# Attention scores in quarters of the array, plain products following their neighbours' tiling, and normalisations moved from GpSimd to ScalarE

## What is computed

```
# block 1, per sequence (H=16 heads of 8, R=8 values per head)
xn = LN(x); q, k, v, qv = four linear maps of xn
score = softmax(q k^T)                       # 16 heads, 512 x 512
out = score v ; comp = softmax over R of ([qv, out] Ws^T) ; out = sum(comp * out)
y = x + Wf out ; y = y + Wr2 relu(Wr1 LN(y)) ; x = LN(x + y)
# block 2, two layers (8 heads of 64, window 64 and the one before)
q, k = l2norm and rotary of h wqkv ; o = local softmax(8 q k^T + mask) v
x = x + wo o ; h = LN(shift(x)) ; x = x + w2 (a * gelu(g)), a, g = w1 h
# at the end x = LN(x_in + x)
```

## Time and profile before

| | |
|---|---|
| median of 3 runs | 1379.37 us (1377.97 to 1383.18) |
| profiled execution | 1383.29 us, its span 1381.5 us |
| TensorE busy | 1247.4 us (90%) |
| VectorE, GpSimd, ScalarE busy | 971.1, 901.7, 803.1 us |
| mean granted TensorE clock | 0.978 |

### The profile page before, as it was taken

One profiled execution on the slowest core, in us unless ns is written; L12 is line 12 of the kernel. 1 busy time (PEld: TensorE's weight loads), 2 busy tenths in 40 slices (PEclk: granted clock), 3 DMA queues, 4 the chain that ended last, 5 costly groups with the idle time before them and its releaser, 6 DMA issues.

```text
span 1381.5 us, 42047 instructions
## 1 busy us (share of the span) xinstructions
PE 1247.4 (90%) x17410; PEld 886.4 (64%) x17410; DVE 971.1 (70%) x1524; ACT 803.1 (58%) x1087; POOL 901.7 (65%) x886
## 2 busy tenths in 40 slices
PE   1689998999999999999999999999999999887885
PEld 1256765666867577666867577675767667565664
DVE  4777489788588876887678776877668673746452
ACT  1256765676656666666656666666656665544442
POOL 4003685778558783878657794778748693979373
PEclk9999999999999999999999999999999999998997
DMA  3410031112101121012111121012201001010100
GB/s 133 157 48 27 11 108 21 25 20 84 41 23 28 47 67 35 19 27 82 43 23 25 42 70 39 18 29 72 52 23 25 10 19 24 17 20 20 32 20 16
DMA packets 112972, 56.70 MB, mean 41 GB/s; under 512 B 82534, under 2 KB 105360, under 8 KB 112784
## 3 DMA queue, kind: packets, MB, share of 16 engines
q1 hardware_dynamic: 108288, 48.52, 13.5%
q10 hardware_dynamic: 4500, 5.51, 1.2%
HBM read 20.18 MB, written 14.68 MB: 25 GB/s over the span
## 4 chain that ended last, share of the span: by engine, by line
PE 77%; POOL 7%; DVE 6%; ACT 5%; issue 3%; DMA 1%; ACTq 1%; SPq 0%; POOLq 0%; DVEq 0%
PE pair L577 66%; PE pair L580 11%; POOL work L1130 3%; DVE gm L1013 2%; POOL rn L1130 2%; ACT probs L775 2%; ACTq L807 1%; ACT L775 1%; DVE o_tok L894 1%; ACT p_t L775 1%; DMA h<-yb 0%; DVE wm L1076 0%; DMA parts_scratch<-shared 0%; ACT work L775 0%; DVE wexp L894 0%
## 5 line engine op out<-in xcount | busy, mean ns | idle before, releaser
L1013 DVE TENSOR_REDUCE gm<-pair 128x2 f32<-128x1024 f32 x256 | 304.2, 1217 | 77.0 <-PE pair L577 74.6
L775 ACT ACTIVATE probs<-pair 128x1024 f32<-128x1024 f32 x256 | 253.8, 1024 | 40.9 <-PE pair L577 28.3
L577 PEld LDWEIGHTS pair<-vt,probs 128*64 128x64 f32 x8192 | 251.0, 138 | 34.5 <-issue 27.5
L577 PE MATMUL pair<-vt,probs 128*64 128x65 f32 x8192 | 268.0, 224 | 0.7 <-ACT gt L775 0.7
L577 PE MATMUL pair<-wqkv,h_t 128*128 128x512 f32 x384 | 188.5, 615 | 3.0 <-ACT h_t L775 1.4
L1130 POOL TENSOR_TENSOR rn<-rn,neg_half 128x16 f32<-128x16 f32 x64 | 187.6, 2932 | 5.3
L1130 POOL TENSOR_TENSOR work<-work 128x1024 f32<-128x1024 f32 (+1 forms) x65 | 151.3, 2328 | 1.0 <-DVE work L894 0.9
L894 DVE TENSOR_TENSOR work<-pair,rot 128x1024 f32<-128x1024 f32 x128 | 150.1, 1214 | 0.0
L775 ACT ACTIVATE raw<-pair 128x260 f32<-128x260 f32 x128 | 49.6, 388 | 142.0 <-PE pair L577 141.9
L1130 POOL TENSOR_TENSOR work<-work,rn 128x1024 f32<-128x1024 f32 x64 | 121.8, 1904 | 4.8
L577 PE MATMUL pair<-h_t,w 128*114 128x256 f32 (+1 forms) x384 | 110.2, 411 | 5.4 <-ACT probs L775 2.0
(11 more groups left out here) (146 smaller groups left out, 2367.4 us busy)
## 6 DMA issues: line engine op xcount, KB each, us to landing
v_mix<-v_nat SPq DMA_DIRECT2D x112, 128.0 KB, 2.8
parts_scratch<-shared SPq DMA_DIRECT2D x16, 384.0 KB, 2.6
k_stack<-parts_scratch SPq DMA_DIRECT2D x64, 96.0 KB, 2.2
q_stack<-parts_scratch SPq DMA_DIRECT2D x64, 96.0 KB, 2.3
parts_scratch<-shared SPq DMA_DIRECT2D x16, 256.0 KB, 2.7
x_in<-in_x SPq DMA_DIRECT2D x8, 256.0 KB, 2.7
parts_scratch<-shared SPq DMA_DIRECT2D x16, 128.0 KB, 2.5
h<-yb SPq DMA_DIRECT2D x64, 32.0 KB
```

The source lines that it names most:

```text
L577: return pe.matmul(b_out, lhsT, rhs, start=start, stop=stop, skip_group_check=True)
L775: return act.activation(dst, src, fn, **kw)
L1013: m = dve.tensor_reduce(gm[:, g % 2, j, :, s % 2], bank("max", b, s, j), AX, ALU.max, negate=True)
```

## The change

1. **Quarters.** `max`, `st` now issue each product as two column halves (`halves`), so that a task is four matmuls on 64 x 64 quarters, the form that `s` has already.
2. **Halves by neighbourhood.** A plain product is issued whole, or as two column halves (128 x 64) if the fixed-form task before it on TensorE is of the 128 x 64 kind (or, after a quarter task, the one that follows is). `gturn` reads 40 columns instead of 8, so that it has the 128 x 64 form too.
3. **The planner** knows three tilings (`TILING`), adds 93 ns to a start where the tiling changes (`RETILE`), shifts the rank of a task that would change it by -0.82 (`STAY`), lets ScalarE and VectorE be free 115 and 90 ns before their result is there, and has new offsets in `TAKEN` and new durations. So every engine's order is new.
4. **Normalisations.** `ln*_norm` goes to ScalarE as `Identity(scale * x + bias)`. GpSimd's `ln*_rstd` makes the bias too (minus mean times inverse root): four instructions instead of two.
5. **Loads.** The loads for block 1 go from ScalarE's queue to SyncE's (`load_search`); rotary tables and scales move to the 15 `layer_loads`, issued by SyncE in five groups after the last `stack` of sequence 0. A `warm` activation loads ScalarE's exponential table at the start.

```diff
+TILING = {"pv": "columns", "o": "columns", "h_turn": "columns", "gturn": "columns", "max": "both", "st": "both", "s": "both",
+          "x_turn": "whole", "att_turn": "whole", "n2_turn": "whole", "qkT": "whole", "pT": "whole", "oT": "whole",
+          "n_turn": "whole", "out_turn": "whole", "out_back": "whole"}
+RETILE = 93
+STAY = -0.82
+def retiles(tiling, wanted):
+    return tiling == "both" if wanted is None else tiling is not None and tiling != wanted
 TAKEN = {
-    "rem": -9.0, "ma": -8.98, "qk_feat": -8.56, "cos": -8.5, "weight": -8.19, "lsub": -7.11, "qk": -6.98,
...
+    "ln2_norm": -9.0, "rowmax": -8.88, "n_turn": -8.62, "lnl_rstd": -7.97, "wsub": -5.25, "mg": -0.09, "pT": 0.1,
...
+        lag = {"ACT": 115, "DVE": 90}.get(engine, 0)
+        self.info[name] = (engine, ns - lag, [a for a in after if a], take, frees, land + lag, table)
...
-                key = (max(start, now[engine]), rank[name])
+                other = engine == "PE" and retiles(tiling, TILING.get(name[0]))
+                key = (max(start, now[engine]), rank[name] + STAY * other)
...
+                if retiles(tiling, wanted):
+                    start += RETILE
+                    tiling = None
+                tiling = wanted or tiling
...
+        for k in (1, -1):
+            tiling = None
+            for name in self.orders["PE"][::k]:
+                tiling = TILING.get(name[0]) or (tiling if tiling != "both" else None)
+                self.halved.setdefault(name, tiling and tiling == "columns")
+                if self.halved[name] is None:
+                    del self.halved[name]
...
-            add(("max", b, s, j), "PE", 250, [("stack", b, 0, g), ("stack", b, 1, g), quad_before("gsplit", g, 2),
+            add(("max", b, s, j), "PE", 220, [("stack", b, 0, g), ("stack", b, 1, g), quad_before("gsplit", g, 2),
...
-    add(("ln3_rstd", b), "POOL", 1360, [("ln3_stats", b)])
-    add(("ln3_norm", b), "POOL", 3130, [("ln3_rstd", b)] + [n("ysum", b - 2, LAYERS - 1, hf) for hf in range(2)])
+    add(("ln3_rstd", b), "POOL", 1950, [("ln3_stats", b)])
+    add(("ln3_norm", b), "ACT", 1500, [("ln3_rstd", b)] + [n("ysum", b - 2, LAYERS - 1, hf) for hf in range(2)])
...
-        gb = sb("gb", [P, 2, T, 2, 2, 2], BF16)
+        gb = sb("gb", [P, 2, 8 * T + 32], BF16)
...
+                def halves(dst, lhsT, rhs, start=True, stop=True):
+                    for c0 in range(0, lhsT.shape[-1], 64):
+                        c1 = min(c0 + 64, lhsT.shape[-1])
+                        m = mm(dst[c0:c1], lhsT[:, c0:c1], rhs, start, stop)
+                    return m
...
+                    product = halves if p.halved.get(name) else mm
...
-                        m = mm(z, wqk[a], xf[:, :])
+                        m = product(z, wqk[a], xf[:, :])
...
-                            m = mm(z[:, r, :], qs[rr, s, j * P:(j + 1) * P], ks[rr, s, :])
+                            m = halves(z[:, r, :], qs[rr, s, j * P:(j + 1) * P], ks[rr, s, :])
...
-                            m = mm(z[:, r, :], ks[rr, s, j * P:(j + 1) * P], qs[rr, s, :])
+                            m = halves(z[:, r, :], ks[rr, s, j * P:(j + 1) * P], qs[rr, s, :])
...
+                def normal(dst, src, tiles, rstd):
+                    for j in tiles:
+                        m = A(dst[:, j, :], src[:, j, :], ACT.Identity, scale=rstd[:, 0, j:j + 1], bias=rstd[:, 1, j:j + 1])
+                    return m
...
+                    if kind == "warm":
+                        act.wait_ge(s_fills, 1)
+                        m = A(warmed[:, :], neg_half[:, 0:1], ACT.Exp)
...
-                        if name == ("gcopy", 0, 0):
-                            for dst, src in layer_loads:
-                                act.dma_start(dst, src).then_inc(s_layers, 16)
...
+                def scales(dst, mom, name):
+                    n, (r, nb) = dst.shape[2], (dst[:, 0, :], dst[:, 1, :])
+                    pool.tensor_scalar(r, mom[:, :, 1], EPS, None, ALU.add).then_inc(sem(name), 1)
+                    pool.tensor_scalar(nb, mom[:, :, 0], -1.0, None, ALU.mult).then_inc(sem(name), 1)
+                    pool.wait_ge(*upto(*name, short=2))
+                    TT(r, r, neg_half[:, 0:n], ALU.pow).then_inc(sem(name), 1)
+                    pool.wait_ge(*upto(*name, short=1))
+                    return TT(nb, nb, r, ALU.mult)
...
+                    elif kind == "load_layers":
+                        k, = ix
+                        for a in range(2):
+                            sp.wait_ge(*upto("stack", 0, a, QUADS - 1))
+                        for dst, src in layer_loads[3 * k:3 * k + 3]:
+                            sp.dma_start(dst, src).then_inc(s, 16)
```

More of the change, by code:

```diff
@@ L94, in order @@
         self.orders = {e: [] for e in engines}
-        self.bank_of, self.before, self.starts = {}, {}, {}
+        self.bank_of, self.before, self.starts, self.halved = {}, {}, {}, {}
         free, freed_by = [0.0] * 8, [None] * 8
@@ L110, in room @@
             return best and (best[0][0], best[1])
-        ends, gives, table = {}, {}, None
+        ends, gives, table, tiling = {}, {}, None, None
         waiting = {}
@@ L170, in order @@
         assert all(not n for n in waiting.values()), [k for k, n in waiting.items() if n][:9]
+        for k in (1, -1):
[5 more added lines that the diff above has]
+                    del self.halved[name]
         return now
 def plan_setup(p):
+    p.rank = -5.0
+    p.add(("load_first", 0), "ACT", 4000, land=2400)
+    p.rank = -4.8
+    p.add(("warm", 0), "ACT", 250, table="exp")
+    p.rank = -0.5
+    p.add(("load_search", 0), "SP", 4400, land=3400)
+    p.rank = 0.1
+    for k in range(5):
+        p.add(("load_layers", 0, k), "SP", 1400, [("stack", 0, a, QUADS - 1) for a in range(2)], land=6000)
     p.rank = -2.0
-    p.add(("weigh", 0), "DVE", 800)
+    p.add(("weigh", 0), "DVE", 700, [("load_first", 0)])
     p.rank = -1.9
@@ L248, in plan_search @@
         add(("gsplit", b, g), "POOL", 500, [("rowmax", b, *sj) for sj in here] + [quad_before("gturn", g, 2)])
-        add(("gturn", b, g), "PE", 230, [("gsplit", b, g), quad_before("gstack", g, 1)], "one", ("gcopy", b, g))
+        add(("gturn", b, g), "PE", 224, [("gsplit", b, g), quad_before("gstack", g, 1)], "one", ("gcopy", b, g))
         add(("gcopy", b, g), "ACT", 570, [("gturn", b, g)])
@@ L275, in plan_search @@
     step(1.02)
[L276 removed]
+    add(("att_turn", b), "PE", 440, [("attsum", b, hf, j) for hf in range(2) for j in range(T)] + [n("m1", b - 1, 1)],
         "one", ("att_feat", b))
@@ L319, in plan_local @@
             first = ("x_next", b, l - 1, hf) if l else ("ln3_norm", b)
-            add(("h_turn", b, l, hf), "PE", 500, [first, ("tables", 0), half_before("ma", l, hf, 2, 2)], "one", ("h_feat", b, l, hf))
+            add(("h_turn", b, l, hf), "PE", 494, [first, ("tables", 0), *[("load_layers", 0, k) for k in range(5)], half_before("ma", l, hf, 2, 2)], "one", ("h_feat", b, l, hf))
             add(("h_feat", b, l, hf), "ACT", 381, [("h_turn", b, l, hf)])
@@ L403, in transfers @@
         return (2 if kind == "v_mix" else 3) - (not more)
-    return {"spill": 3, "stack": 2, "gstack": 2}.get(kind, 1)
+    return {"spill": 3, "stack": 2, "gstack": 2, "load_layers": 3, "load_search": 9}.get(kind, 1)
 RAWC = RV + 1
@@ L559, in build @@
             (w_all[:, 2 * D:], t["w_all"][:, 2 * D:7 * D]),
-            (tab, t["tables"]), (flat[:, 1536:2048], t["scales"].partition_broadcast(P)),
         ]
-        layer_loads = [(mask[:, :, :], t["mask"])]
+        layer_loads = [(tab, t["tables"]), (flat[:, 1536:2048], t["scales"].partition_broadcast(P)), (mask[:, :, :], t["mask"])]
         for l in range(LAYERS):
@@ L1220, in _ @@
                         pool.wait_ge(*upto("ln3_stats", b))
-                        m = inverse_root(rstd2[:, :], moments2, name)
-                    elif kind == "ln3_norm":
-                        pool.wait_ge(*upto("ln3_rstd", b))
-                        if b > 1:
-                            for hf in range(2):
-                                pool.wait_ge(*upto("ysum", b - 2, LAYERS - 1, hf))
-                        m = normal(x_b[b % 2], s1, range(T), moments2, rstd2)
+                        m = scales(rstd2[:, :, :], moments2, name)
                     elif kind == "rnorm":
```

221 lines of the change are left out of this document (111 added, 110 removed).

## The result

The changed kernel takes 1418.84 us (median of 4 runs, 1416.09 to 1425.41) against 1381.11 for the kernel before on the same chip (4 runs): a ratio of 1.0273 [1.0245, 1.0302]. The forecast was 1344 us with a range from 1306 to 1374; the change has the wrong sign, and the time lies far outside the range. The profiled execution took 1425.4 us, its span is 1423.6.

The account below looks back on a forecast made before the run. TensorE's work was taken to bound the middle, latencies of chains the start and end. Terms -20 - 8 - 6 - 1 = -35 us took the profiled 1383.3 to 1348, or 1344 us against the 1379.4 median; range 1306 to 1374.

Parts of the forecast that it names:

- The new order: TensorE's list: the new planner would leave 60 fewer changes of tiling, -8 us, bounds +23 to -35.
- The prediction's own sign of being wrong: Profile after: the period stays above 155 us, or the first dense stretch starts over 5 us later than before.
- Quarters and halves: TensorE, old order: new forms cut changes of tiling from 875 to 709, saving leaving and entering costs, -20 us.
- Rival C: TensorE's score tasks: each shows one 104 ns load, 53 us over 512 tasks, time 1397 us; chance 0.06.
- Rival A: TensorE's list: the order does not keep tiling changes away; 1362 to 1386 us, say 1371; chance 0.21.
- Normalisations: Moved from GpSimd to ScalarE: hidden by TensorE's work in the middle, gaining at the end of the program, -6 us.
- rival D: ScalarE: waiting normalisations hold PSUM evictions that TensorE needs, +36 us, 1380, no change; chance 0.05.
- Loads: Program start: table load leaves the path, -2.5 us, against later gstack loads on SyncE's queue, +1.5; together -1 us.

Follow-up runs that it names:

- Experiment 5: The kernel before's planner with the new forms, only st planned at 218 ns instead of 250, orders made anew; 1482.53 us, ratio 1.0741 to the kernel before.
- experiment 1: The kernel before with its five orders unchanged and only the new forms (quarters, halves, gturn on 40 columns); 1356.01 us, ratio 0.9802.
- 12: New forms, block 1 loads on SyncE's queue, warm, and other TAKEN offsets whose plan still repeats, against the kernel before; 1359.19 us, ratio 0.9819.
- number 3: The changed kernel with its new orders, normalisations and loads, but the old forms: products whole, scores as 128 columns, gturn on 8; 1425.74 us, ratio 1.0302.
- 8: The changed kernel with STAY at nothing and the old TAKEN offsets, planned anew; 1430.27 us, ratio 1.0357 to the kernel before.
- 7: The kernel before with new forms and normalisations on ScalarE, planned there by the old planner with old offsets; 1446.29 us, ratio 1.0479.
- 6: The changed kernel with normalisations planned and run on GpSimd, every order made anew; 1436.27 us, ratio 1.0394 to the kernel before.
- experiment 2: The kernel before with new forms and normalisations moved to ScalarE's list at their planned starts, other orders kept; 1398.2 us, ratio 1.0108.
- Experiment 11: The kernel before's order with new forms, block 1 loads on SyncE's queue and warm; 1361.36 us, ratio 0.9836 to the kernel before.

## Why the prediction was wrong

**The step that failed is "The new order", -8 us with bounds of +23 and -35.** It priced an order by one property, its number of changes of form, because that was what the planner's edit spoke of. The number came out between its bounds (779, where it took 709 - 60), and by its own price of 0.14 us the miss is 130 x 0.14 = 18 us, of which 10 lie above the 709 of the old order. The rest of the cost is waits. The sum had order, normalisations and loads at -8 - 6 - 1 = -15 us together; measured, they cost 1418.84 - 1356.01 = 63. The old plan has settled into a cycle of one sequence in which TensorE was busy 152 of 157 us, and no rule of the planner asks for that. Whether the offsets in `TAKEN` were chosen with it is not on record; with `TAKEN` empty the same planner plans an end at 1460 us instead of 1292. Experiment 5 shows that the cycle is lost with one number, and 126 us with it, while the work stays the same. A new order had to be costed as a new draw, with a bound on the slow side from the row that was at hand: TensorE's 90%, kept by that one order. The prediction's own sign of being wrong, a period above 155 us, is what the steps of 158 to 181 us show.

**The plan told it.** The kernel computes its plan before it runs, so the planned starts of any version can be had without a run. The planned ends of block 2 are 149 us apart each time before, and 154, 164, 161, 171 after. The planned end of the whole program tells as much: 1292 us before and 1355 after, although most of TensorE's tasks are planned shorter. The table has it beside what was measured in the profiled executions. Tasks is the sum over TensorE's list of the distance from a task's start to the next one's, taken at the tenth percentile of all tasks of the same kind, form, and form before and behind; rest is the span less that sum, so waits and slow stretches.

| kernel | planned end | span | tasks | rest |
|---|---|---|---|---|
| before | 1292 | 1381.5 | 1201 | 181 |
| 1, new forms, old order | 1292 | 1356.3 | 1170 | 187 |
| 12, other offsets, repeats | 1290 | 1356.4 | 1170 | 186 |
| after | 1355 | 1423.6 | 1177 | 247 |
| 3, after with old forms | 1355 | 1426.2 | 1205 | 221 |
| 8 | 1369 | 1432.5 | 1158 | 274 |
| 7 | 1370 | 1444.6 | 1159 | 286 |
| 6 | 1372 | 1435.3 | 1178 | 258 |
| 5 | 1388 | 1478.4 | 1158 | 320 |

Computed in the same way, without a run, the old plan keeps its cycle with `st` at 248 to 251 ns and has lost it at 245 and 252. The plans that repeat end at 1290 to 1292, the others at 1355 to 1388, and the measured spans follow in nearly the same order. Number 5 has the least work on TensorE and the longest rest. From number 3 to the changed kernel the tasks lose 28 us and the rest gains 26. The split depends somewhat on how finely tasks are grouped: for the change as a whole it is -24 in the tasks and +66 in the rest here, and other groupings put the rest's growth between +43 and +72.

Part of the rest is the clock. Two successive short stretches in the middle of the changed kernel, the first with gaps in TensorE's work:

```profile
853.00:861.20 8.20, 6.07 (x108) 3.26 (x104) 8.16 (x12) 4.63 (x7) 7.87 (x8) 1.00 0.18 36
861.20:868.00 6.80, 6.10 (x24) 3.85 (x22) 4.96 (x6) 5.61 (x8) 6.63 (x4) 0.50 0.01 2
```

The granted clock goes to 0.50, the 1.2 GHz level, at 861.2 us, after 8.2 us in which TensorE was busy 6.07. The mean clock gives the size: 1423.6 x (1 - 0.946) = 77 us less 65 x 0.33 = 21 of the start, so 55 us of full-speed time lost, against 1381.5 x (1 - 0.978) = 30 before. That is up to 25 of the 66. The first 65 us are left out on both sides, because the 1.00 that the earlier trace rows has there for the kernel before is not what its tasks show: the two score tasks at 56.50 take 1.04 us, and two of them in the middle

```profile
648.87 0.61 PE L577 MATMUL pair<-q_stack,k_stack 50*128 50x512 bf16 x4
```

so that start too ran slowly. How the 66 divides between the places of the moved normalisations and the offsets stays open, since every plan that separates them is a new draw too.

**Quarters and halves, -20.** Right in kind, low in size: -28. The prices that can be read again hold. TensorE after, in order of time:

```profile
802.91 0.41 PE L615 MATMUL pair<-q_stack,k_stack 50*64 50x512 bf16 x4
803.25 1.98 PE L615 MATMUL pair<-wqkv,h_t 128*128 128x512 f32 x4
805.07 1.04 PE L625 MATMUL pair<-ident,wexp 128*128 128x128 f32 x8
806.04 0.41 PE L615 MATMUL pair<-q_stack,k_stack 50*64 50x512 bf16 x4
806.38 1.94 PE L615 MATMUL pair<-wqkv,h_t 128*64 128x512 f32 x8
808.14 0.22 PE L615 MATMUL pair<-v_mix,p_t 128*64 128x65 f32 x1
...
811.36 0.63 PE L615 MATMUL pair<-q_stack,k_stack 50*64 50x512 bf16 x8
811.91 0.28 PE L615 MATMUL pair<-vt,probs 128*64 128x65 f32 x2
```

The two score tasks at 811.36 take 0.55 us up to the `pv`. One that leaves its form takes 0.34 (802.91 to 803.25), which leaves 0.21 for the first. The same four-instruction product after a quarter task takes 1.82 us whole (803.25 to 805.07) and 1.76 as halves (806.38 to 808.14), against 1.71 within its form: entering costs 0.11 whole and 0.05 halved, as in the sum (0.095 and 0.05). The table has the tasks of experiment 1 at 31 us less, so, as far as that table can tell, the missing eight lies in the tasks and not in waits. Two things the sum left out work this way: the old order enters quarters 64 times (`s`, 1.3 us at its own 0.02) and `gturn`'s form 32 times without a price. The clock may hold up to 4 us: by mean clocks experiment 1 lost 1356.3 x (1 - 0.968) - 65 x 0.27 = 26 us of full-speed time after the start, where before lost 30. The rest stays open; the 0.055 for entering a transpose was the term with least behind it.

**Rival C, exposed loads of quarters**, is refuted: 0.21 to 0.22 us per score task where it needed 0.30. The Trainium skill (TensorEngine Tiling (Array Packing), Feature Incompatibilities) says that column tiling goes without Fast Weight Load. This case's trace agrees that the narrower load is not a quicker one: the 64-column score loads take 105 to 107 ns after, where the 128-column ones took 94 to 95 before. Behind 512 columns none of that shows, by the same 0.21 to 0.22 us.

**Rival A, the order does not keep the changes away**, is half true: the order brought back 70 of the 166. Its price was wrong, as that of the term was: it put such an order at 1386 us at most.

**Normalisations, -6.** The loads on the engines were right: GpSimd -121 us (said -118), and ScalarE +73 in experiment 2 (875.6 less 802.8; said +71). The further 18 us after lie within its 18 more table loads of 1.28 us (23 us). An instruction is 0.48 us alone and 0.39 from start to start (said 0.37):

```profile
L822 ACT ACTIVATE gate<-h,rstdl 128x128 f32<-128x128 f32 x64 | 28.1, 487 | 26.3 <-POOL rstdl L1209 26.2
...
L1209 POOL TENSOR_TENSOR rstdl<-rstdl,neg_half 128x2 f32<-128x2 f32 x48 | 34.4, 718 | 4.0
```

What was wrong is "nothing is gained there and TensorE's work hides the cost". In the old order it costs 42 us, by the mechanism of **rival D**: ScalarE, not full, stands before a normalisation while evictions queue behind it. That D's 36 us are so close is partly luck: it took 1 us of waiting for each of 72 normalisations and half of it as felt, where the waits are 48 / 72 = 0.67 us and most of them are felt. D had 0.05 and deserved far more; its own argument against, 108 of 157 us, is about load, and the mechanism is about places. The gain of 6 at the end is not there either: the last two steps are 257.5 us in experiment 2 and 248.9 in experiment 1.

**Loads, -1.** Nothing speaks against it, and it is too small for these runs to confirm. The start after, all engines:

```profile
3.86 1.28 ACT L822 ACT_TABLE_LOAD   x1 [3.86 <-issue]
...
56.41 1.07 PE L615 MATMUL pair<-q_stack,k_stack 50*64 50x512 bf16 x8 [7.06 <-DMA q_stack<-gt]
```

The table load left the path, the first transposes begin at 9.4 instead of 16.6 us, and the wait for `gstack` grew from 4.17 to 7.06, within its bounds; TensorE reaches the same task at 56.41 instead of 56.50. Experiment 11, with a part of the moved loads, cannot be told from nothing either. Moving the loads of block 2 was not tried by itself; numbers 5 and 7 lose the time without it.

## What to carry to other kernels

When an edit replaces an order made by a greedy list scheduler, price the order as a whole and not by the property that the edit speaks of. See first whether the old one repeats and whether the new one does (its planned starts tell, here 149, 149, 149 against 154, 164, 161), and compare the planned ends (here 1292 against 1355 us). Put a slow side on the forecast that is as wide as the idle time the old order had kept away. Cheaper forms of work should be tried first in the old, frozen order: there they gave 28 us, and in the new one 4 to 7. An engine with room to spare still holds others up where an instruction that waits stands ahead of the evictions in its list.

## What was not expected of the hardware

- A plain product of 512 float32 columns that enters a new form costs 0.11 us more whole and 0.05 as two column halves, and halving lengthens nothing: a `v` product, half of such a group, takes 0.86 us within its form either way.
- The granted clock falls to 0.50 in the middle of a dense program, behind stretches with short waits: at 861.2 us, for 6.8 us, after 8.2 us with 6.07 busy. In the old order it stayed at 1.00 through the middle (309 to 1095 us).
- A clock of 1.00 in the view of stretches need not mean full speed: in the first 65 us of the kernel before it says 1.00, and two score tasks take 1.04 us there against 0.61 in the middle.
- A normalisation of 128 x 128 float32 on ScalarE with scale and bias from columns takes 0.48 us alone, but four in a row take 1.65 us.
